# A windowed attention kernel: one wait of VectorE split up, TensorE's loop begun two groups sooner, one pair of statistics moved

## The reference

```
h = group_norm(x, 32 groups of 4 channels)          # statistics over a whole image
h = roll(h, (-3, -3)) in rows and columns
q, k, v = w_qkv @ h + b_qkv                         # 1x1 convolution, 3 x 128 rows
per window of 7x7 pixels, per head (8 heads of 16 channels):
    out = softmax(q k^T / 4) v                      # 49 x 49 scores
x + roll(out, (3, 3))
```

## Time and profile before

| | us |
|---|---|
| median of 3 runs | 1049.76 |
| lowest and highest | 1048.53, 1051.95 |
| profiled execution, its own time | 1047.67 |
| its span | 1045.9 |
| TensorE busy in the span | 976.6 (93%) |
| VectorE busy | 785.8 (75%) |
| ScalarE busy | 697.1 (67%) |
| GpSimd busy | 595.6 (57%) |

### The profile page before, as it was taken

One profiled execution on the slowest core, in us unless ns is written; L12 is line 12 of the kernel. 1 busy time (PEld: TensorE's weight loads), 2 busy tenths in 40 slices (PEclk: granted clock), 3 DMA queues, 4 the chain that ended last, 5 costly groups with the idle time before them and its releaser, 6 DMA issues. The chain is left out here.

```text
span 1045.9 us, 104658 instructions
## 1 busy us (share of the span) xinstructions
PE 976.6 (93%) x46595; PEld 770.2 (74%) x46595; DVE 785.8 (75%) x1532; ACT 697.1 (67%) x1297; POOL 595.6 (57%) x1067
## 2 busy tenths in 40 slices
PE   0589999999979999999997999999999999999995
PEld 0367777777767777777775777787878787777774
DVE  7656888889856888888984888788877777777762
ACT  2455777777756777777774777777777777777752
POOL 1444666666555665666663666566656665666651
PEclk9988999999998999999997999999999999999995
DMA  9201111111110111111110000000000000000000
GB/s 382 119 18 52 47 45 61 61 54 39 61 62 31 61 40 53 61 61 46 46 62 31 31 31 15 31 31 31 15 31 31 31 19 27 31 31 24 22 33 34
DMA packets 29925, 52.05 MB, mean 50 GB/s; under 512 B 3650, under 2 KB 28868, under 8 KB 29764
## 3 DMA queue, kind: packets, MB, share of 16 engines
q1 hardware_dynamic: 29892, 51.59, 14.0%
HBM read 25.89 MB, written 25.69 MB: 49 GB/s over the span
## 5 line engine op out<-in xcount | busy, mean ns | idle before, releaser
L571 DVE TENSOR_REDUCE neg_max<-psum 100x16 f32<-100x784 f32 x256 | 249.5, 975 | 172.3 <-PE psum L729 172.3
L375 ACT ACTIVATE probs_t<-psum,exp_scale 128x800 f32<-128x800 f32 x256 | 237.5, 928 | 85.6 <-PE psum L746 55.4
L283 POOL TENSOR_SCALAR k_hi<-k 128x392 f16<-128x392 f32 x128 | 67.5, 527 | 243.3 <-PE psum L746 242.0
L746 PE MATMUL psum<-q_masks,k_hi 32*64 32x100 f16 x8192 | 190.3, 208 | 15.8 <-DVE inv L576 12.4
L729 PE MATMUL psum<-k_hi,q_masks 32*128 32x49 f16 x8192 | 199.2, 180 | 2.3 <-issue 1.2
L305 POOL TENSOR_TENSOR stage<-mixed,image 128x343 f32 (+7 forms) x256 | 162.4, 653 | 48.4 <-issue 37.4
L729 PEld LDWEIGHTS psum<-k_hi,q_masks 32*128 32x128 f16 x8192 | 176.4, 91 | 12.0 <-issue 1.6
L729 PE MATMUL psum<-k_lo,q_masks 32*128 32x49 f16 x4096 | 183.6, 179 | 0.6 <-issue 0.6
L746 PEld LDWEIGHTS psum<-q_masks,k_hi 32*64 32x64 f16 x8192 | 153.7, 106 | 39.1 <-issue 16.9
L564 DVE TENSOR_SCALAR q_masks<-q_halves,even_odd 128x800 f16<-128x800 f16 x256 | 162.8, 678 | 0.1
L729 PEld LDWEIGHTS psum<-k_lo,q_masks 32*128 32x128 f16 x4096 | 161.8, 92 | 0.8 <-issue 0.8
(11 more groups left out here) (120 smaller groups left out, 1909.9 us busy)
## 6 DMA issues: line engine op xcount, KB each, us to landing
out_dram<-stage SPq DMA_DIRECT2D x64, 224.0 KB, 2.0
out_dram<-stage SPq DMA_DIRECT2D x64, 168.0 KB, 1.9
image<-in_x_dram SPq DMA_DIRECT2D x32, 224.0 KB, 2.6
image<-in_x_dram SPq DMA_DIRECT2D x1, 6104.0 KB, 27.2
image<-in_x_dram SPq DMA_DIRECT2D x34, 168.0 KB, 2.5
image<-in_x_dram SPq DMA_DIRECT2D x6, 896.0 KB, 9.4
image<-in_x_dram SPq DMA_DIRECT2D x1, 728.0 KB, 14.0
w_nat<-in_L_conv_w_qkv_dram SPq DMA_DIRECT2D x1, 192.0 KB, 2.5
```

The source lines that it names most:

```text
L375: nc.scalar.activation(probs_t[:, 2 * u:2 * u + 2, :, :].rearrange("p h a q -> p h (a q)"), psum[:, COL_BANKS, 0:PAIRS * ROWS2], ACT.Exp, ...
L571: nc.vector.tensor_reduce(neg_max[:, par, 2 * j:2 * j + 2, :], psum[0:ROWS2, ROW_BANKS, 0:GT] .rearrange("p h (w k) -> p h w k", k=TOK), A ...
L746: last = nc.tensor.matmul(psum[side, COL_BANKS.start + h % 2, a * ROWS2:(a + 1) * ROWS2], k[rows, par, w, :], q_masks[rows, par, low + w * ...
```

## The change

On VectorE the statistics of images 2 and 3 run eight steps as written-out code in place of four. Each pair of steps waits for only those bands that its chunks read; the wait for all 16 bands stands four steps later than before. On TensorE the loop starts with step 2 in place of step 4. For its register waits to be positive, `join_done` and `mixed_done` are raised by one at VectorE's start, and every wait on them asks for one more. The statistics of image 1 start in step 2 in place of step 1, three chunks in each of steps 2 and 3. On ScalarE the wait for `scales_ready` stands behind step -2, which only normalises group 0.

```diff
@@ gpsimd
             def add_image(g, t, half):
-                pool.wait_ge(mixed_done, g + 1)
+                pool.wait_ge(mixed_done, g + 2)
@@ scalar
-            act.wait_ge(scales_ready, 1)
-
...
-                wait(act, join_done, g)
+                wait(act, join_done, g + 1)
...
-            for g in range(-2, 4):
+            step(-2, -1, 0)
+            act.wait_ge(scales_ready, 1)
+            for g in range(-1, 4):
                 step(g, g // 2, g & 1)
@@ vector
+            dve.sem_inc(join_done, 1)
+            dve.sem_inc(mixed_done, 1)
...
-                wait(dve, mixed_done, g)
+                wait(dve, mixed_done, g + 1)
...
-                dve.wait_ge(join_done, g + 1)
+                dve.wait_ge(join_done, g + 2)
...
             step(0, 0, 0)
+            step(1, 0, 1)
             dve.wait_ge(loaded[1], 32)
-            step(1, 0, 1, (0, 1), BANDS * BAND)
-            step(2, 1, 0, (2, 3), BANDS * BAND)
-            step(3, 1, 1, (4, 5), BANDS * BAND)
+            step(2, 1, 0, (0, 1, 2), BANDS * BAND)
+            step(3, 1, 1, (3, 4, 5), BANDS * BAND)
...
                 first = b * BANDS - 1
-                dve.wait_ge(loaded[b + 1], 32 * -(-2 * STAT // BAND))
-                two_steps(first, 0, at)
-                dve.wait_ge(loaded[b + 1], 32 * -(-4 * STAT // BAND))
-                two_steps(first + 1, 2, at)
+                for n in range(4):
+                    dve.wait_ge(loaded[b + 1], 32 * -(-(2 * n + 2) * STAT // BAND))
+                    two_steps(first + n, 2 * n, at)
                 dve.wait_ge(loaded[b + 1], 32 * BANDS)
-                with dve.Fori(2, CHUNKS // 2) as n:
+                with dve.Fori(4, CHUNKS // 2) as n:
                     two_steps(n + first, 2 * n, at)
@@ tensor
-                wait(pe, mixed_done, g - 2)
+                wait(pe, mixed_done, g - 1)
...
-                wait(pe, join_done, g)
+                wait(pe, join_done, g + 1)
...
-                    pe.wait_ge(mixed_done, g)
+                    pe.wait_ge(mixed_done, g + 1)
...
-            for g in range(-1, 4):
+            for g in range(-1, 2):
                 step(g, g & 1)
-            with pe.Fori(2, GROUPS // 2 - 1) as n:
+            with pe.Fori(1, GROUPS // 2 - 1) as n:
```

## The result

| | before, us | after, us |
|---|---|---|
| median of 4 runs | 1050.12 | 1021.66 |
| lowest and highest | 1048.53, 1051.95 | 1016.95, 1024.01 |
| profiled execution, its own time | 1047.67 | 1024.01 |
| its span | 1045.9 | 1022.1 |

The ratio is 0.9723, 95% interval 0.9681 to 0.9765. The forecast was 1022.0 us and held. A second set of runs of the changed kernel, five beside nine of the kernel before, gave 1021.3 us, ratio 0.9713 (0.9691 to 0.9735). The execution that was profiled is the slowest of the four shown, so the two profiled spans differ by 23.8 us where the medians differ by 28.5.

What follows compares the result with a forecast made beforehand. TensorE, busy 93% of the span, was taken as the bound; 20.5 + 5.9 + 0.9 = 27.3 us off the profiled 1047.67 gave 1020.4, off the median 1022.5; forecast 1022.0 us, eight-in-ten range 1016 to 1030.

Steps and rivals of the forecast that it cites:

- The removed wait: VectorE's wait for all 16 bands at two changes of image: without it both stretches fall to 7.43 us, 20.5 us off.
- The step from wait to stretch: At the changes of image, worth read from the stretches (9.96 and 10.55 us), half-clock matmuls behind the standstill included.
- TensorE's loop: At the head, begun at step 2: steps 4 and 5 are no longer first-run code, 5.9 us off.
- the two stretches that the prediction named: At the head, 76.72 to 89.26 and 89.26 to 97.46 us, within steps 4 to 6: 12.54 and 8.20 fall to 7.43.
- The low bound: At TensorE's head: the half-clock phase turns up anyway, 3.3 us lost, leaving 2.6 us of gain.
- the head gives nothing: Rival, 20%: a loop's first-pass fetches are no different and half clock falls elsewhere at the head; 1029.3 or 1028.4 us.
- The price of a fetch: TensorE's instruction fetches at the head: 13.9 us for 14 fetches, 1.0 us each.
- The jump back: TensorE's loop; rival, 1%: each jump back stalls, 1.4 us at most, and code run the first time is free; 1029.8 us.
- The rival of the lost loop body: Rival, 4%: TensorE's loop body no longer stays held, every pass fetches again; 1084 us, with all six fetches near 1390.
- The start: ScalarE's first normalise no longer waits for the scales; the shift carries through to the first projection: 0.9 us off.
- The statistics: VectorE's chunks moved from step 1 to steps 2 and 3 are covered by idle time: cost 0; uncovered 1.1 us.
- The tail: Same code, 9 fetches, but page borders and clock may shift: taken as 0, bounded by -3 and +3 us.

Runs made afterwards that it cites:

- the body of four steps: The changed kernel with four steps in TensorE's loop body, 31 passes in place of 62 of two: 1540.53 us, ratio 1.4676.

## Why the prediction held, point by point

**The removed wait, 20.5 us.** Measured alone 20.7 (17.9 to 23.5), and both stretches at 7.43 us in the trace. Nothing took its place. The step from wait to stretch, that the half-clock time belongs to the stop, is what made the number: TensorE's two standstills alone would have given 12.4.

**TensorE's loop, 5.9 us.** Measured alone 6.6 (4.3 to 8.8). In the profiled executions the five head stretches took 49.3 to 51.0 us with the loop from step 4 (four executions) and 43.0 to 46.0 with the loop from step 2 (five), 5.1 less on average; the two stretches that the prediction named took 20.7, 21.4, 20.8 and 18.7 in the four, against 14.9 now, 5.5 on average. The size was right and its parts were not. The prediction put 2.5 us down to the gaps and "the rest mostly the half-clock time"; at full clock the same two stretches cost 5.9 us in one execution and 3.8 in another. The low bound, 2.6 us if the half-clock time came anyway, lies under all four. The rival "the head gives nothing" has fallen: in none of the five executions does the record of the clock show half clock at the head behind the turn of maxima in step 4. The price of a fetch, 1.0 us (13.9 us by 14 fetches, of which one came ahead of the five stretches), fits here, where 6 fewer fetches gave 5.1 to 6.6 us; it was too low for the body of four steps, 1.3.

**The jump back.** The Trainium skill ("Runtime: NRT & Kernel Launch", Instruction fetch mechanics) says that a taken branch to a page outside a two-page window forces a fetch. By that rule the loop should have lost. The earlier trace rows had spoken against two pages being all that TensorE holds, and the changed kernel's middle shows no fetch either. The body of four steps shows the forced fetch itself at work, with 388 fetches in 1400 us and 3.86 us at the jump shown: the rule comes true once the body is larger than what is held, which lies between two and four steps of this kernel. The rival of the lost loop body was a real one; its 1390 us at worst, for 62 passes of six fetches, was low, as the body of four steps took 1540 us with about as many.

**The start, 0.9 us.** ScalarE's start follows `shift_c` by 0.20 us in place of 1.07, as forecast. That it "carries through" is shown by the first projection, 0.87 us sooner behind `shift_c` in all eight executions, by the average up to the first turn of maxima, and by the 1.9 us (0.5 to 3.2) of the part alone.

**The statistics, 0.** Measured 1.0002 (0.9985 to 1.0019). With the statistics alone the slack in step 2 was used up to the last tenth, as the row had said, and the maximum was not late. In the changed kernel's own trace the maxima of steps 2 and 3 have idle time ahead of them, 2.22 and 0.40 us: most of step 2 ran at half clock there (59.43 to 66.20 us at 0.50).

**The tail, 0 with 3 us either way.** 1.6 us more in the profiled pair. From the turn of group 121's maxima to the end of the span the five executions with the loop from step 2 took 65.8 to 68.1 us, the four with it from step 4 65.6 to 66.4, so the bound held. The prediction read the 3.4 us between the runs as clock phases of which some would go. The record does not show it: the changed kernel's four runs lie 7 us apart and its five in the second set 3.5, the 24 runs of the kernel before 8.2.

**Where luck had a part.** The sum of the prediction is 27.3 us off the profiled execution. The medians differ by 28.5, the two profiled spans by 23.8: runs of one kernel differ by several microseconds at the head and the tail, so that the agreement of the forecast with the median to 0.3 us is closer than its terms could promise.

## What to carry to other kernels

Read the worth of a wait from the stretch of the bounding engine around it, clock and all, and not from the wait: here 7.5 us of VectorE's waiting were 10 us of the kernel, and the same transfer awaited 5 us later in the engine's order was 1.1. Wait for what the next instruction reads, and put the wait right ahead of it. In this kernel of many short matmuls each written-out step of TensorE was paid for once (some 3.5 us), and a loop's body had to stay small enough to be held: two steps cost nothing to repeat, four cost half the kernel's time again.

## What was not expected of the hardware

Half-clock time and the gaps of first-run code do not simply add. The kernel with TensorE's loop alone ran its first head stretch with no gap at all:

```profile
47.03:59.22 12.19, 12.19 (x359) 9.18 (x357) 5.94 (x13) 5.42 (x11) 3.33 (x6) 1.00 0.01 4
```

The column of the clock says 1.00 there, but the lengths of one and the same matmul in that stretch and in the next say otherwise:

```profile
54.27 0.53 PE L704 MATMUL psum<-xn_hi,w_lo 128*128 128x392 f16 x1
...
63.80 0.33 PE L704 MATMUL psum<-xn_hi,w_lo 128*128 128x392 f16 x1
```

So that stretch ran at the lower clock, which the column misses ahead of the first record of it (59.0 us in this trace): read it at the start of a kernel together with a matmul's length. The same stretch of the changed kernel, at full clock (its record begins at 45.8 us), takes 9.90 us with TensorE busy for 7.78. The half-clock window of the earlier trace rows, 81.90 to 88.60, is alike: busy for 6.56 of 6.70 us. That the fetches keep up because the matmuls take longer is a likely reason, but no run here tests it.

A jump back to code that is no longer held cost 2.6 to 4.3 us, against 1.9 us at most for a gap in the straight code of the same run and 1.4 in the earlier trace rows. Why it costs more was not tried.
